# Tower layers over two tiles at a time, and one more sum on ScalarE, in an interaction network with a ranking tower

## The chip, the cores and the metric

The kernel runs on one core of a Trainium2 chip. The metric is the device time of one execution in microseconds, the median of several.

## The reference

For 1024 samples, 32 embedding rows of 16 numbers are gathered, three cross layers are applied, and a small tower follows. Everything is fp32.

```python
# x0, e: (1024, 32, 16); W0: (32, 32, 64); W1, W2: (32, 64, 64)
for W in (W0, W1, W2):
    xk = relu(einsum('bmd,bhd,mhk->bkd', x0, xk, W))
    outs.append(sum(xk, axis=2))            # over d
h = concatenate(outs + [dense_ctx], axis=1)  # 3 * 64 + 16 columns
h = maximum(h @ W_top1 + b_top1, 0)          # 208 x 512
h = maximum(h @ W_top2 + b_top2, 0)          # 512 x 256
y = h @ W_top3                               # 256 x 1
```

## The kernel before

The batch is cut into 16 streams of 64 samples (COLS = 64 x 16 = 1024 columns of sample and d). Two streams, an even one a (slot a) and an odd one b (slot b), make a tile of 128 samples (TB). A layer of a stream is a sum over 16 chunks (4 in layer 0): VectorE or GpSimd multiplies a rolled copy of x0 (`rolled`) by xk into `zd` or `zg`, and TensorE multiplies the product by the chunk's weights into `acc`, the two halves of 512 columns into two halves of the partitions of one bank. VectorE makes two chunks with one instruction into one of three buffers (ZD_BUFS), GpSimd one chunk into one of four. Layer 0 has one more term, from the squares of x0 that ScalarE makes (`squares`). Layer 0 of every stream uses the bank `stage`, layers 1 and 2 a bank for each slot.

ORDER is the order of the phases, written by hand: for m = 0 to 6, with a = 2m + 2 and b = a + 1, it is (b - 2, 2, 0), (a, 0, 0), (b - 2, 2, 1), (a, 1, 0), (b, 0, 0), (a, 1, 1), (b, 1, 0), (a, 2, 0), each (stream, layer, part). TensorE, VectorE and GpSimd all go through it. A pass of the loop over m is these eight phases, and the last phase (15, 2, 0) stands alone.

After a layer ScalarE copies relu(acc) to `xk_ps` for VectorE and `xk_sb` for GpSimd (`evacuate`, L486). It then sums relu over d for each sample with 32 activations of 16 columns that accumulate (`sum_d`, L465). Where `by_act` says no, it writes relu to `relu_ab` (L498) and VectorE reduces it (`reduce_d`, L391). In the passes of m this is layer 0 of slot a alone. Before a stream starts, ScalarE copies `base` (x0 repeated) for VectorE (`base_to_ps`, L439). Each phase of TensorE waits until the sums over its bank are done.

The tower of a tile runs as three blocks in TensorE's queue, in a bank of its own (`mlp`): `mlp2(m - 1)` in the phase (a, 1, 0), `mlp3(m - 1)` in (a, 1, 1), `mlp1(m)` in (b, 1, 0) after its fourth item. ScalarE takes each result out (`h2_to_sb`, `y_to_sb`, `h1_to_sb`). The sums come to it by six copies (`zsum_to_sb`). Tile 7 has code of its own at the end.

SP's queue issues, for each stream, a store of the gathered rows to a scratch (L269), a load of `base` (L287), and 16 loads of rolled tiles (L296). Each of these waits until the user before it (the same slot's layer 2) has used the tile (L294). GpSimd issues the gathers between its products.

## Time and profile before

| | |
|---|---|
| median of 3 runs | 613.49 us (612.25 to 613.73) |
| the profiled execution | 612.87 us |
| its span | 611.1 us, mean granted clock 0.992 |
| TensorE busy | 559.8 us |
| VectorE busy | 549.2 us |
| GpSimd busy | 451.9 us |
| ScalarE busy | 406.4 us |

The span is the time from the first to the last instruction, so 1.8 us of the profiled execution lie around it. The rows further down name engines as PE (TensorE), PEld (its weight loads), DVE (VectorE), ACT (ScalarE), POOL (GpSimd) and SPq (SP's queue). Each fp32 matmul is recorded twice, as two records.

### The profile page before, as it was taken

To read this page: it belongs to the slowest core of one execution; us is meant where nothing else is said; L and a number is where in the kernel's file an instruction comes from. 1 tells how busy PE (TensorE), PEld (TensorE's weight loads), DVE (VectorE), ACT (ScalarE), POOL (GpSimd) and SP (SyncE) were. 2 spreads that over 40 slices of the span, in tenths; PEclk is the share of its full clock that TensorE was granted. 3 is DMA by queue.
4 is the path that set the end of the run, shared out by engine and by line. 5 is a ranking of instruction groups with operands and counts; after the bars stand their busy time and mean duration, and the time that the engine had idled before them with its cause. 6 is when DMAs were issued, how large, how long until landed. Compare 5 with 4: busy or idle time off the path is not lost.

```text
span 611.1 us, 9367 instructions
## 1 busy us (share of the span) xinstructions
PE 559.8 (92%) x2668; PEld 201.3 (33%) x2668; DVE 549.2 (90%) x267; ACT 406.4 (67%) x2717; POOL 451.9 (74%) x347
## 2 busy tenths in 40 slices
PE   0058889999999999999999999999999999999997
PEld 0012322323333343344333343343334333333344
DVE  0077799999999999999999999999999999999990
ACT  0031506677877688768867688778867688678851
POOL 6748788878888878888888888888887874214630
PEclk9998899999999999999999999999999999999999
DMA  6297969693598819895597819894598819891000
GB/s 173 81 386 260 392 238 393 230 398 123 168 399 295 326 38 365 286 388 185 168 400 286 335 43 390 289 401 138 193 380 284 330 50 388 294 413 46 2 1 1
DMA packets 54263, 152.11 MB, mean 249 GB/s; under 512 B 9697, under 2 KB 18913, under 8 KB 54210
## 3 DMA queue, kind: packets, MB, share of 16 engines
q1 hardware_dynamic: 46018, 149.39, 65.3%
q0 software_dynamic: 8192, 2.11, 2.8%
q8 instruction: 21, 0.34, 0.2%
q14 instruction: 32, 0.26, 0.1%
HBM read 147.26 MB, written 4.20 MB: 248 GB/s over the span
## 4 chain that ended last, share of the span: by engine, by line
PE 82%; DVE 6%; POOL 5%; issue 3%; DMA 2%; ACT 1%; SPq 1%; DVEq 0%; POOLq 0%
PE acc L606 74%; DVE zd L415 6%; POOL emb L332 4%; PE mlp L643 2%; PE acc L615 2%; DMA rolled<-x_scratch 2%; PE mlp L634 1%; PE mlp L635 1%; POOL zg L344 1%; SPq L296 1%; PE mlp L650 1%; ACT xk_sb L486 0%; DMA emb<-tables_in,index 0%; ACT xk_ps L486 0%; DMA x_scratch<-emb 0%
## 5 line engine op out<-in xcount | busy, mean ns | idle before, releaser
L415 DVE TENSOR_TENSOR zd<-rolled,xk_ps 128x2048 f32<-128x2048 f32 (+1 forms) x246 | 535.4, 2248 | 14.1 <-PE acc L606 11.6
L606 PE MATMUL acc<-zd,w_sb 128*64 128x512 f32 x1700 | 388.8, 597 | 8.5 <-DVE zd L415 8.5
L332 POOL DMA_INDIRECT emb<-tables_in,index x256 | 244.5, 955 | 77.2 <-issue 64.7
L344 POOL TENSOR_TENSOR zg<-rolled,xk_sb 128x1024 f32<-128x1024 f32 x87 | 207.2, 2384 | 57.1 <-ACT xk_sb L486 41.6
L606 PEld LDWEIGHTS acc<-zd,w_sb 128*64 128x64 f32 x1700 | 120.5, 138 | 254.9 <-issue 219.5
L465 ACT ACTIVATE relu_ab<-acc 128x16 f32<-128x16 f32 x1152 | 190.9, 302 | 3.8 <-PE acc L606 3.5
L465 ACT ACTIVATION_READ_ACCUMULATOR relu_ab<-acc 128x1 f32 x1152 | 191.6, 329 | 0.1
L486 ACT ACTIVATE xk_sb<-acc 64x512 f32<-64x512 f32 x128 | 76.4, 597 | 57.5 <-PE acc L606 55.0
L606 PE MATMUL acc<-zd,w 128*64 128x512 f32 x256 | 62.8, 610 | 36.5 <-DVE zd L415 36.5
L606 PE MATMUL acc<-zg,w_sb 128*64 128x512 f32 x348 | 90.9, 600 | 2.9 <-POOL zg L344 2.8
L486 ACT ACTIVATE xk_ps<-acc 64x512 f32<-64x512 f32 x126 | 71.8, 570 | 28.0 <-PE acc L606 25.1
L443 ACT ACTIVATE xk_sb<-base 128x1024 f32<-128x1024 f32 x16 | 16.9, 1057 | 57.0 <-PE acc L606 28.7
L606 PEld LDWEIGHTS acc<-zd,w 128*64 128x64 f32 x256 | 18.6, 140 | 71.4 <-issue 69.3
L606 PEld LDWEIGHTS acc<-zg,w_sb 128*64 128x64 f32 x348 | 24.5, 137 | 50.5 <-issue 44.3
L439 ACT COPY xk_ps<-base 128x512 f32<-128x512 f32 x30 | 16.6, 587 | 23.7 <-DMA base<-x_scratch 18.7
L415 DVE TENSOR_TENSOR zd<-rolled,base 128x1024 f32<-128x1024 f32 x4 | 4.9, 1230 | 27.7 <-DMA rolled<-x_scratch 27.7
L615 PE MATMUL acc<-xk_sb,w 128*64 128x512 f32 x64 | 18.3, 648 | 0.0
L643 PEld LDWEIGHTS mlp<-h,wt 128*128 128x128 f32 x112 | 13.0, 191 | 5.7 <-issue 5.7
L391 DVE TENSOR_REDUCE zpart<-relu_ab 128x32 f32<-128x512 f32 x12 | 8.1, 678 | 7.0 <-ACT relu_ab L498 7.0
L643 PE MATMUL mlp<-h,wt 128*128 128x128 f32 x112 | 14.4, 281 | 0.0
L498 ACT ACTIVATE relu_ab<-acc 128x512 f32<-128x512 f32 x12 | 7.2, 598 | 7.3 <-PE acc L606 7.0
L515 ACT ACTIVATE h<-mlp,bt 128x128 f32<-128x128 f32 x28 | 8.0, 368 | 5.7 <-PE mlp L635 5.7
(45 smaller groups left out, 88.0 us busy)
## 6 DMA issues: line engine op xcount, KB each, us to landing
rolled<-x_scratch SPq DMA_DIRECT2D x256, 512.0 KB, 10.5
base<-x_scratch SPq DMA_DIRECT2D x16, 512.0 KB, 3.7
emb<-tables_in,index POOLq DMA_INDIRECT x256
x_scratch<-emb SPq DMA_DIRECT2D x32, 128.0 KB, 5.9
w_sb<-w_in SPq DMA_DIRECT2D x2, 512.0 KB, 4.6
wt<-wtop_in SPq DMA_DIRECT2D x1, 512.0 KB, 6.6
wt1a<-wtop_in SPq DMA_DIRECT2D x1, 256.0 KB, 5.2
w<-w0a_in SPq DMA_DIRECT2D x1, 160.0 KB, 2.3
```

The source lines that it names most:

```text
L332: pool.indirect_dma_start(emb[:, i % 2, c * DIM:(c + 1) * DIM], None, tables, bass.IndirectOffsetOnAxis(index[:, g:g + 1].bitcast(U32), 0) ...
L344: nc.gpsimd.tensor_tensor(zg[:, n % ZG_BUFS, :], rolled[:, s, j, :], xk_sb[:, s, :], ALU.mult).then_inc(zg_ready, 1)
L391: nc.vector.tensor_reduce(zpart[:, t % 2, layer, s, :], relu_ab[:, s, :].rearrange("p (b d) -> p b d", d=DIM), AX_X, ALU.add).then_inc(red ...
L415: nc.vector.tensor_tensor(zd[:, n % ZD_BUFS, 0:w, :], rolled[:, s, j:j + w, :], repeated(layer_in, w), ALU.mult).then_inc(zd_ready, 1)
L439: nc.scalar.copy(xk_ps[:, s, h * HALF:(h + 1) * HALF], base[:, h * HALF:(h + 1) * HALF]).then_inc(base_ps, 1)
L443: nc.scalar.activation(xk_sb[:, i % 2, :], base[:, :], ACT.Square).then_inc(squares_ready, 1)
L465: end = nc.scalar.activation(relu_ab[:, s, cols], acc[:, bank, cols], ACT.Relu, accum_out=zpart[:, t % 2, layer, s, b:b + 1])
L486: nc.scalar.activation(dst[copy * MAPS:(copy + 1) * MAPS, s, h * HALF:(h + 1) * HALF], acc[h * MAPS:(h + 1) * MAPS, bank, :], ACT.Relu).th ...
L515: nc.scalar.activation(h1[:, c, :], mlp[:, c * TB:(c + 1) * TB], ACT.Relu, bias=bt1[:, c:c + 1]).then_inc(h1_sb, 1)
L606: end = nc.tensor.matmul(acc[h * MAPS:(h + 1) * MAPS, bank, :], weights, z[:, h * HALF:(h + 1) * HALF], start=(j + c == 0), stop=(i == len ...
L615: nc.tensor.matmul(acc[h * MAPS:(h + 1) * MAPS, bank, :], w0[:, L0CH, :], xk_sb[:, s, h * HALF:(h + 1) * HALF], start=False, stop=False)
L643: end = nc.tensor.matmul(mlp[:, c * TB:(c + 1) * TB], wt2[:, k, c * P:(c + 1) * P], h1[:, k, :], start=(k == 0), stop=(k == H1 // P - 1))
```

## The change

The tower takes two tiles (256 columns, TW) at a time for tiles 0 to 5, and tile 6 alone as before. The first layer has 4 x 256 columns of output, twice the bank, so it is done in two halves: part 0 in the phase (b, 1, 0) and part 1 in (a, 2, 0), both in odd m, with ScalarE emptying the bank between them. The second and third layer of the pair are done in the next pass, which has an even m > 0. ScalarE sums layer 0 of slot a as well, from stream 2 on, so VectorE's reductions in the passes of m are gone. To make room, `index` is computed in place in `ids_sb`, `h2` lies in one half of `relu_ab`, and all sums of streams after 0 write their unread output to the other half.

```diff
+TW = 2 * TB
+PAIRS = (TILES - 2) // 2
 def by_act(stream, layer):
     if stream < 2:
         return layer == 2
-    return (layer > 0 or stream % 2 == 1) and (stream, layer) != (STREAMS - 1, 2)
+    return (stream, layer) != (STREAMS - 1, 2)
...
-        index = sb("index", [P, STREAMS * GATHERS], I32)
+        index = ids_sb[:, 1:]
...
-        z01 = sb("z01", [P, TB])
+        z01 = sb("z01", [P, TW])
-        h1 = sb("h1", [P, H1 // P, TB])
-        h2 = sb("h2", [P, H2 // P, TB])
+        h1 = sb("h1", [P, H1 // P, TW])
+        h2 = relu_ab[:, 0, :].rearrange("p (c b) -> p c b", b=TW)
...
             def reduce_d(q):
                 stream, layer, _ = ORDER[q]
                 s, t = stream % 2, stream // 2
-                if layer == 0 and s == 0 and t > 1:
-                    dve.wait_ge(zsum_sb, ZSUM_COPIES * (t - 1))
...
             def sum_d(stream, layer):
-                before = phase_before(stream, layer)
-                if by_act(*before):
-                    act.wait_ge(summed, act_sums_to(*before))
+                unread = relu_ab[:, min(stream, 1), :]
+                if stream == 0:
+                    act.wait_ge(reduced, sums_to(0, 1))
                 else:
-                    act.wait_ge(reduced, sums_to(*before))
+                    act.wait_ge(reduced, sums_to(1, 1))
+                    act.wait_ge(summed, act_sums_to(stream, layer) - 1)
...
+            def h1_to_sb(p, part):
+                act.wait_ge(h1_done, 2 * p + part + 1)
+                for x in range(2):
+                    c = 2 * part + x
+                    nc.scalar.activation(h1[:, c, :], mlp[:, x * TW:(x + 1) * TW], ACT.Relu,
+                                         bias=bt1[:, c:c + 1]).then_inc(h1_sb, 1)
...
             for t in range(1, TILES):
                 a, b, m = 2 * t, 2 * t + 1, t - 1
+                first_of_two, second_of_two = m % 2 == 0 and m > 0, m % 2 == 1
                 base_to_ps(a)
                 wait_end(a - 2, 2)
                 squares(a)
                 sum_d(a - 2, 2)
                 evacuate(a, 0)
                 base_to_ps(b)
+                sum_d(a, 0)
                 wait_end(b - 2, 2)
                 squares(b)
                 sum_d(b - 2, 2)
-                if m > 0:
-                    h2_to_sb(m - 1)
+                if first_of_two:
+                    h2_to_sb(m // 2 - 1)
                 evacuate(b, 0)
                 zsum_to_sb(m)
-                if m > 0:
-                    y_to_sb(m - 1)
+                if first_of_two:
+                    y_to_sb(m // 2 - 1)
                 sum_d(b, 0)
                 evacuate(a, 1)
-                h1_to_sb(m)
+                if second_of_two:
+                    h1_to_sb(m // 2, 0)
+                elif m == TILES - 2:
+                    one_h1_to_sb()
                 sum_d(a, 1)
                 evacuate(b, 1)
                 sum_d(b, 1)
+                if second_of_two:
+                    h1_to_sb(m // 2, 1)
...
+            def mlp1(p, part):
+                if part == 0:
+                    pe.wait_ge(zsum_sb, ZSUM_COPIES * (2 * p + 2))
+                    if p > 0:
+                        pe.wait_ge(y_ready, p)
+                else:
+                    pe.wait_ge(h1_sb, 4 * p + 2)
+                for x in range(2):
+                    c, dst = 2 * part + x, mlp[:, x * TW:(x + 1) * TW]
+                    nc.tensor.matmul(dst, wt1a[:, c * P:(c + 1) * P], z01[:, :], start=True, stop=False)
+                    end = nc.tensor.matmul(dst, wt1b[:, c * P:(c + 1) * P], z2d[:, p * TW:(p + 1) * TW],
+                                           start=False, stop=True)
+                end.then_inc(h1_done, 1)
...
             for m in range(TILES - 1):
-                q = 6 + 8 * m
+                q, p = 6 + 8 * m, m // 2
+                first_of_two, second_of_two = m % 2 == 0 and m > 0, m % 2 == 1
                 for x in range(3):
                     phase(q + x)
-                phase(q + 3, {1: lambda: mlp2(m - 1)} if m > 0 else {})
+                phase(q + 3, {1: lambda: mlp2(p - 1)} if first_of_two else {})
                 phase(q + 4)
-                phase(q + 5, {4: lambda: mlp3(m - 1)} if m > 0 else {})
-                phase(q + 6, {3: lambda: mlp1(m)})
-                phase(q + 7)
-            m = TILES - 2
-            phase(len(ORDER) - 1, {1: lambda: mlp2(m), 4: lambda: mlp3(m), 6: last_sums})
+                phase(q + 5, {4: lambda: mlp3(p - 1)} if first_of_two else {})
+                if m == TILES - 2:
+                    phase(q + 6, {3: one_mlp1})
+                else:
+                    phase(q + 6, {3: lambda: mlp1(p, 0)} if second_of_two else {})
+                phase(q + 7, {3: lambda: mlp1(p, 1)} if second_of_two else {})
+            phase(len(ORDER) - 1, {1: one_mlp2, 4: one_mlp3, 6: last_sums})
```

`mlp2`, `mlp3`, `h2_to_sb` and `y_to_sb` are as before with TW in place of TB. `one_mlp1`, `one_mlp2`, `one_mlp3` and their copies are the old code for tile 6. `zsum_to_sb(m)` writes its columns of the wide `z01`.

## Rows read from the trace of the kernel before

**Rows 1.** The page: busy time of each engine.

```profile
PE 559.8 (92%) x2668; PEld 201.3 (33%) x2668; DVE 549.2 (90%) x267; ACT 406.4 (67%) x2717; POOL 451.9 (74%) x347
```

**Rows 2.** By stretch (m = 0, 3): length; busy PE, PEld, DVE, ACT, POOL; clock; DMA.

```profile
84.69:153.17 68.48, 65.43 (x298) 20.85 (x298) 68.48 (x34) 41.38 (x238) 56.98 (x47) 1.00 0.77 281
...
290.14:358.63 68.49, 68.49 (x335) 24.88 (x336) 67.52 (x33) 53.38 (x372) 59.21 (x47) 1.00 0.75 273
```

**Rows 3.** TensorE's waits in m = 0 (84.69 to 153.17): total, times, longest.

```profile
PE acc L606 <- DVE zd L415: 3.9, 12, 0.9
```

**Rows 4.** VectorE's waits for TensorE in m = 3 (290.14 to 358.63).

```profile
DVE zd L415 <- PE acc L606: 0.6, 1, 0.6
```

**Rows 5.** Timeline of TensorE, m = 3: start, us, instruction, count.

```profile
332.64 0.60 PE L606 MATMUL acc<-zd,w_sb 128*64 128x512 f32 x2
333.17 2.05 PE L643 MATMUL mlp<-h,wt 128*128 128x128 f32 x16
335.15 0.65 PE L606 MATMUL acc<-zd,w 128*64 128x512 f32 x2
...
339.50 3.60 PE L606 MATMUL acc<-zd,w_sb 128*64 128x512 f32 x16
342.93 1.03 PE L606 MATMUL acc<-zg,w_sb 128*64 128x512 f32 x4
...
346.79 0.60 PE L606 MATMUL acc<-zd,w_sb 128*64 128x512 f32 x2
347.32 0.60 PE L650 MATMUL mlp<-h,wt 128*1 128x128 f32 x4
347.85 0.65 PE L606 MATMUL acc<-zg,w_sb 128*64 128x512 f32 x2
```

**Rows 6.** Timeline of VectorE, m = 3, around its reduction.

```profile
326.18 0.68 DVE L391 TENSOR_REDUCE zpart<-relu_ab 128x32 f32<-128x512 f32 x1
326.78 2.27 DVE L415 TENSOR_TENSOR zd<-rolled,xk_ps 128x2048 f32<-128x2048 f32 x1
```

**Rows 7.** Table by stretch for the sums (L465) alone, m = 3.

```profile
290.14:358.63 68.49, 27.07 (x320) 1.00 0.75 273
```

**Rows 8.** Timeline of ScalarE, m = 3; in brackets idle time before, and releaser.

```profile
326.78 1.11 ACT L439 COPY xk_ps<-base 128x512 f32<-128x512 f32 x2 [0.96 <-DMA base<-x_scratch]
...
339.71 2.44 ACT L486 ACTIVATE xk_sb<-acc 64x512 f32<-64x512 f32 x4 [3.03 <-PE acc L606]
...
347.96 0.25 ACT L526 COPY z2d_y<-mlp 1x128 f32<-1x128 f32 x1 [1.82 <-PE mlp L650]
```

**Rows 9.** Timelines of VectorE, then TensorE, m = 4, around (11, 1, 0).

```profile
417.25 4.47 DVE L415 TENSOR_TENSOR zd<-rolled,xk_ps 128x2048 f32<-128x2048 f32 x2
...
417.25 5.75 PE L606 MATMUL acc<-zd,w_sb 128*64 128x512 f32 x26
```

**Rows 10.** Timelines of VectorE's waits in m = 1 and 4, and TensorE ahead of the second.

```profile
155.08 2.29 DVE L415 TENSOR_TENSOR zd<-rolled,xk_ps 128x2048 f32<-128x2048 f32 x1 [0.15 <-PE acc L606]
...
429.04 2.29 DVE L415 TENSOR_TENSOR zd<-rolled,xk_ps 128x2048 f32<-128x2048 f32 x1 [0.73 <-PE acc L606]
...
427.06 0.65 PE L606 MATMUL acc<-zd,w_sb 128*64 128x512 f32 x2
```

**Rows 11.** Timeline of VectorE, its waits for a rolled tile, m = 3 and 5.

```profile
333.84 2.29 DVE L415 TENSOR_TENSOR zd<-rolled,xk_ps 128x2048 f32<-128x2048 f32 x1 [0.39 <-DMA rolled<-x_scratch]
...
470.69 2.29 DVE L415 TENSOR_TENSOR zd<-rolled,xk_ps 128x2048 f32<-128x2048 f32 x1 [0.26 <-DMA rolled<-x_scratch]
```

**Rows 12.** Timeline of SP's queue, m = 3: start and time of issuing.

```profile
296.57 12.51 SPq L296 DMA_DIRECT2D rolled<-x_scratch  x16
309.12 1.07 SPq L269 DMA_DIRECT2D x_scratch<-emb  x2
322.84 0.52 SPq L287 DMA_DIRECT2D base<-x_scratch  x1
```

**Rows 13.** Table by stretch between store and base load, m = 3; columns of rows 2.

```profile
309.00:322.80 13.80, 13.80 (x68) 4.65 (x66) 13.80 (x7) 9.10 (x71) 12.21 (x10) 1.00 0.92 351
```

More of the change, by code:

```diff
@@ L464, in sum_d @@
                     cols = slice(b * DIM, (b + 1) * DIM)
-                    end = nc.scalar.activation(relu_ab[:, s, cols], acc[:, bank, cols], ACT.Relu,
+                    end = nc.scalar.activation(unread[:, cols], acc[:, bank, cols], ACT.Relu,
                                                accum_out=zpart[:, t % 2, layer, s, b:b + 1])
@@ L492, in evacuate @@
                 if before and by_act(*before):
-                    act.wait_ge(summed, act_sums_to(*before))
+                    act.wait_ge(summed, act_sums_to(stream, layer))
                 elif before:
@@ L503, in zsum_to_sb @@
                 act.wait_ge(summed, act_sums_to(2 * m + 1, 2))
-                if m > 0:
-                    act.wait_ge(h1_done, m)
-                for layer, dst in enumerate([z01[0:MAPS, :], z01[MAPS:P, :], z2d[0:MAPS, m * TB:(m + 1) * TB]]):
+                if m > 1:
+                    act.wait_ge(h1_done, 2 * (m // 2))
+                col = m % 2 * TB
+                for layer, dst in enumerate([z01[0:MAPS, col:col + TB], z01[MAPS:P, col:col + TB],
+                                             z2d[0:MAPS, m * TB:(m + 1) * TB]]):
                     for h in range(2):
@@ new lines, in mlp2, with mlp3 @@
+            def mlp2(p):
+                pe.wait_ge(h1_sb, 4 * (p + 1))
+                for c in range(H2 // P):
+                    for k in range(H1 // P):
+                        end = nc.tensor.matmul(mlp[:, c * TW:(c + 1) * TW], wt2[:, k, c * P:(c + 1) * P],
+                                               h1[:, k, :], start=(k == 0), stop=(k == H1 // P - 1))
+                end.then_inc(h2_done, 1)
+            def mlp3(p):
+                pe.wait_ge(h2_sb, 2 * (p + 1))
+                for k in range(H2 // P):
+                    end = nc.tensor.matmul(mlp[0:1, 0:TW], wt3[:, k:k + 1], h2[:, k, :],
+                                           start=(k == 0), stop=(k == H2 // P - 1))
+                end.then_inc(y_done, 1)
@@ L632, in mlp1, with one_mlp1 @@
+            def one_mlp1():
+                pe.wait_ge(zsum_sb, ZSUM_COPIES * (TILES - 1))
+                pe.wait_ge(y_ready, PAIRS)
                 for c in range(H1 // P):
                     dst = mlp[:, c * TB:(c + 1) * TB]
-                    nc.tensor.matmul(dst, wt1a[:, c * P:(c + 1) * P], z01[:, :], start=True, stop=False)
-                    end = nc.tensor.matmul(dst, wt1b[:, c * P:(c + 1) * P], z2d[:, m * TB:(m + 1) * TB],
-                                           start=False, stop=True)
+                    nc.tensor.matmul(dst, wt1a[:, c * P:(c + 1) * P], z01[:, 0:TB], start=True, stop=False)
+                    end = nc.tensor.matmul(dst, wt1b[:, c * P:(c + 1) * P],
+                                           z2d[:, (TILES - 2) * TB:(TILES - 1) * TB], start=False, stop=True)
@@ L637, in mlp1, with one_mlp2 @@
                 end.then_inc(h1_done, 1)
-            def mlp2(m):
-                pe.wait_ge(h1_sb, 4 * (m + 1))
+            def one_mlp2():
+                pe.wait_ge(h1_sb, 4 * (PAIRS + 1))
                 for c in range(H2 // P):
@@ L643, in mlp2, with one_mlp3 @@
                         end = nc.tensor.matmul(mlp[:, c * TB:(c + 1) * TB], wt2[:, k, c * P:(c + 1) * P],
-                                               h1[:, k, :], start=(k == 0), stop=(k == H1 // P - 1))
+                                               h1[:, k, 0:TB], start=(k == 0), stop=(k == H1 // P - 1))
                 end.then_inc(h2_done, 1)
-            def mlp3(m):
-                pe.wait_ge(h2_sb, 2 * (m + 1))
+            def one_mlp3():
+                pe.wait_ge(h2_sb, 2 * (PAIRS + 1))
                 for k in range(H2 // P):
-                    end = nc.tensor.matmul(y_bank, wt3[:, k:k + 1], h2[:, k, :],
+                    end = nc.tensor.matmul(mlp[0:1, 0:TB], wt3[:, k:k + 1], h2[:, k, 0:TB],
                                            start=(k == 0), stop=(k == H2 // P - 1))
@@ L680, in _ @@
             for c in range(H1 // P):
-                nc.tensor.matmul(last_h1_bank[c], wt1a[:, c * P:(c + 1) * P], z01[:, :], start=True, stop=False)
-            pe.wait_ge(y_ready, m)
+                nc.tensor.matmul(last_h1_bank[c], wt1a[:, c * P:(c + 1) * P], z01[:, 0:TB], start=True, stop=False)
+            pe.wait_ge(y_ready, PAIRS + 1)
             pe.wait_ge(reduced, sums_to(STREAMS - 1, 2))
@@ L691, in _ @@
                 for c in range(H2 // P):
-                    end = nc.tensor.matmul(last_h2_bank[c], wt2[:, k, c * P:(c + 1) * P], h1[:, k, :],
+                    end = nc.tensor.matmul(last_h2_bank[c], wt2[:, k, c * P:(c + 1) * P], h1[:, k, 0:TB],
                                            start=(k == 0), stop=(k == H1 // P - 1))
@@ L697, in _ @@
                 pe.wait_ge(last_h2_sb, k + 1)
-                end = nc.tensor.matmul(last_y_bank, wt3[:, k:k + 1], h2[:, k, :],
+                end = nc.tensor.matmul(last_y_bank, wt3[:, k:k + 1], h2[:, k, 0:TB],
                                        start=(k == 0), stop=(k == H2 // P - 1))
```

46 lines of the change are left out of this document (24 added, 22 removed).

## The prediction

> **What bounds the kernel now.** I read the page's busy shares first: TensorE is busy 92% and VectorE 90% of the span [rows 1]. The table by stretch splits this [rows 2]. In the pass m = 3 TensorE is busy for all 68.49 us and VectorE for 67.52, and the other passes from m = 1 to 5 are like it. In the first pass (m = 0) it is the other way round: VectorE is busy for all 68.48 us and TensorE for 65.43. So two engines are within 1.5% of each other, and the question is not only how much work TensorE loses but when it has it. The waits say the same: in the pass m = 0, which has no second and third tower layer in it, TensorE waits 12 times for VectorE's products [rows 3]; in the pass m = 3 VectorE waits instead, 0.6 us for TensorE [rows 4] and 0.39 for a transfer [rows 11]. The clock is granted in full in both [rows 2], so all TensorE times below are at 2.4 GHz.
>
> **Sizes of the blocks.** TensorE's work in one pass is 74 chunks, as ORDER and CHUNKS have them, and three tower blocks. A chunk (two halves, two records each) takes 0.858 us: 16 records in 3.43 us (339.50 to 342.93) [rows 5], which is 0.429 per 512 columns, and the two halves of a pair run together. In the second tower layer 16 records lie between 333.17 and 335.15 [rows 5]. The records stand 0.1115 us apart (1.98 less the 0.2 up to the next chunk, over 16). Counted from the last chunk's second record (332.64, and 0.43 for its streaming) the block costs TensorE 2.08 us, and 2.13 with the slower start of the chunk behind it. The first layer is the same size, 2.13. The third layer (347.32 to 347.85, last record before it 346.79) costs 0.68 [rows 5]. Of each block some 0.25 to 0.35 us is not streaming.
>
> **What the change takes and gives on TensorE.** With twice the columns I price a record at 0.2158 us: 128 columns take 0.1115 and 512 take 0.429, and a straight line between them gives 0.217. Then half a first layer for two tiles is 8 x 0.2158 + 0.35 = 2.08, the second layer 16 x 0.2158 + 0.35 = 3.80, the third 4 x 0.2158 + 0.25 = 1.11. A pair costs 2.08 x 2 + 3.80 + 1.11 = 9.07 where two tiles cost 2 x (2.13 + 2.13 + 0.68) = 9.88. That is 0.81 less per pair, 2.4 us over three pairs. The block's fixed part is bounded by zero and 0.35, which moves a pair by 0.3 at most in its path below. The Trainium skill's page "TensorE: Matmul & The Clock Gate" (Back-to-back issue gap) gives a sustained spacing of about 81 ns at 128 columns and 131 ns at 512; the rows have 111.5 and 429, so here four times the columns cost 3.8 times and not 1.6 times. By the page's ratio, a record of 256 columns would cost an estimated 0.135 us.
>
> **VectorE and ScalarE.** VectorE loses one reduction per pass: 326.18 to 326.78, 0.60 us [rows 6]. ScalarE gets a sixth sum per pass: 27.07 us for five is 5.41 each [rows 7], less the 0.6 copy that it replaces. ScalarE is busy 53.4 of 68.5 us [rows 2] and would be at about 58, which fits. I followed it in the pass m = 3: it copies base for the odd stream from 326.78 for 1.1 us [rows 8], sums until 333.3, and then squares. TensorE begins that stream's first layer at 335.15, behind the tower's second layer [rows 5]. With that layer gone it could begin at 333.1, so 0.2 us late, at a place where it is about to wait for VectorE anyway. The odd stream's relu copies start at 339.7 after a wait of 3.03 us [rows 8], and are then on time. The copy of y is waited for 1.8 us [rows 8], in passes with a third layer only. I price ScalarE at nothing. Its cover is these waits, and without them it would cost up to 2 us in a pass. GpSimd gets nothing new. VectorE's queue also loses its wait for the z copies, which held nothing.
>
> **When TensorE has the work.** Now a second and third layer for two tiles stand in the passes m = 2, 4, 6 ("first"), both halves of a first layer in m = 1, 3, 5 ("second"). A second pass therefore loses 2.13 + 0.68 = 2.81 us of TensorE work ahead of the middle of the odd stream's layer 1, where TensorE has almost nothing in hand. In the pass m = 4 it starts the third item of (11, 1, 0) at 422.40 (12 steps of 0.429 after 417.25), and VectorE ended that product at 421.72, so the lead is 0.68 [rows 9]. The smallest lead that the trace needs is about 0.06. VectorE has 0.6 us less to do and 2.81 is taken, so TensorE waits 2.81 - 0.62 - 0.6, about 1.6 us, there. In a first pass the long second layer holds VectorE instead, for all three product buffers are then full: the same product starts at 419.44, TensorE had freed its buffer at 418.97, and the tightest that occurs is 0.21 (a start at 429.04 after a release at 428.83, which is 427.06 and four steps, a wait of 0.73) [rows 9, 10]. That leaves 0.26.
>
> So the longest path alternates. From the third product of (b, 1, 0) in a second pass it runs on TensorE, past the two half blocks, into the first pass, past the long second and third layers. There it passes to VectorE's third product of (b, 1, 0), and VectorE works without a wait until the same place of the next second pass. Against before, for one pair:
> - TensorE: +4.16 - 2.13 (two halves for one block), +1.67 (3.80 - 2.13), +0.43 (1.11 - 0.68) = +4.13
> - room at the handover to VectorE -0.26, and at the one back -0.62
> - VectorE: reduction -0.60, its wait of 0.73 gone.
>
> That is +1.92 us per pair. Ahead of it stands the opening. VectorE sets m = 0 and m = 1, and at the handover in m = 1 it is earlier by two reductions, the 0.15 that it waited at 155.08 [rows 10] and the room of 0.62, 1.97 in all; the two halves for one block then give back 2.03. That is +0.06 by the end of m = 1. Then come two pairs of passes (m = 2, 3 and 4, 5), and m = 6, which keeps its own first layer and pays +1.67 + 0.43 = +2.10; TensorE leads from there to the end. Sum: 0.06 + 2 x 1.92 + 2.10 = +6.0 us.
>
> **The transfer.** In a second pass a DMA chain runs beside VectorE: the even stream's 16 rolled tiles are issued from 296.57, as VectorE frees them, the store of the odd stream's scratch queues behind them (309.12), its base load follows at 322.84, and VectorE's second product of (9, 0, 0) waits until 333.84 for its tile [rows 11, 12]. DMA is 92% busy between the store and the base load [rows 13], so I hold the 37.3 us from issue to landing fixed. VectorE then can't use its 0.6 there, nor the 0.39 that it waits already: +1.0 us in m = 3. In m = 5 the wait is 0.26 [rows 11], so +0.86. In m = 1 there is no such wait, but VectorE comes 0.75 earlier, and I add 0.2. Together +2.0. It is between 0 (the chain follows) and 2.0, and I take the whole, for its start is set by VectorE's own releases. The forecast is +8.0 on the profiled execution's 612.87 us, so 620.9; the median of before is 0.6 above that execution, so 621.5.
>
> **Rivals.**
> - The transfers follow VectorE: +6.0, 619.5 us. For it: m = 1, 4 and 6 show no such wait. Against it: the 92%.
> - ScalarE is late as well. Its new sum stands ahead of the squares and of the odd stream's sum, and with a base load that lands at 326.7 it has no idle time until 339. At 1 us in each second pass and 0.5 in the first ones, 624 us. It decides once its relu copies start later than TensorE's end plus the 3.0 us shown.
> - It gets faster: TensorE's lead isn't used up, and its own work sets the time. That is 2.4 us off plus 0.6 for the reduction in m = 0: 610.5 us. It needs VectorE to make its products faster than one per 2.2 us when not held. The pass m = 0 speaks against it, for TensorE waited there and VectorE was still busy without a break [rows 2, 3].
> - Wide records are cheap and the long blocks stay short. With a record of 256 columns no dearer than one of 128, the path per pair is 1.24 x 2 - 2.13 - 2.21 = -1.86, the opening -1.62: 608 us. By the Trainium skill's ratio above it would be an estimated 611. The 3.8 times speaks against both.
>
> **Numbers.** The forecast has 0.5, the following transfers 0.22, late ScalarE 0.13, the two faster rivals 0.07 and 0.03; 0.05 is left for a gain and a loss that meet. The range from 616.5 to 624.5 holds the first three, with fixed parts of the blocks near zero at its low end. 0.3% is 1.8 us, about what this kernel's runs can tell. Faster 0.09, same 0.05, slower 0.86.
>
> **What would show it.** In the changed profile: TensorE waits for VectorE's products in m = 1, 3, 5, 2.7 us for a pair and 1.0 more where the transfer binds (the 1.92 and the 0.81 that it has less to do), and hardly in m = 2, 4, 6; VectorE waits for TensorE by some 4 us in m = 2, 4; passes of unequal length, and no reduction in either; tower blocks of 2.1, 2.1, 3.8 and 1.1 us. TensorE's waits in second passes under 0.5 us would make it wrong, or relu copies of ScalarE as the releaser of TensorE or VectorE.

## The result, and the profile after

The changed kernel takes 620.0 us (618.63 to 621.92, 4 runs) where the one before takes 612.87 (612.08 to 613.73, 4 runs). The ratio is 1.0122, interval [1.0106, 1.0137]: 7.1 us slower. The profiled execution took 621.92 us with a span of 620.1, against 612.87 and 611.1 before, so it is 9.0 us longer, and 1.9 above its own median. The forecast was 621.5, or 620.9 against the profiled 612.87.

The page's busy shares, to set beside [rows 1]:

```profile
PE 561.5 (91%) x2560; PEld 193.4 (31%) x2560; DVE 546.7 (88%) x260; ACT 434.3 (70%) x3137; POOL 451.7 (73%) x347
```

No engine of the two at the top got more work of note. TensorE's 561.5 is 1.7 more, but a record's time contains short waits, so its work is better counted from block sizes, below. VectorE has 2.5 less. Both shares fell because the span grew. ScalarE has 27.9 more. From these shares alone no one could say why it is slower.

The table by stretch of the changed kernel can. Each row is one pass, m = 1 to 6, counted from TensorE's first item of (b - 2, 2, 0); columns as in [rows 2].

```profile
172.38:243.71 71.33, 69.23 (x315) 23.56 (x313) 68.57 (x32) 57.29 (x432) 61.45 (x49) 1.00 0.77 277
243.71:312.48 68.77, 68.64 (x319) 24.18 (x317) 66.45 (x31) 57.36 (x431) 55.59 (x44) 1.00 0.71 256
312.48:382.99 70.51, 69.30 (x315) 23.41 (x313) 68.48 (x32) 57.30 (x432) 61.24 (x47) 1.00 0.78 282
382.99:451.76 68.77, 68.64 (x319) 24.18 (x317) 66.44 (x31) 57.37 (x431) 58.15 (x47) 1.00 0.71 254
451.76:523.99 72.23, 69.31 (x315) 23.37 (x313) 68.57 (x32) 57.29 (x432) 52.82 (x35) 1.00 0.75 277
523.99:594.54 70.55, 70.55 (x334) 26.06 (x332) 67.25 (x31) 57.29 (x433) 27.43 (x12) 1.00 0.43 165
```

Two passes of the kernel before, cut at the same place:

```profile
174.60:243.09 68.49, 68.49 (x334) 24.89 (x332) 67.76 (x33) 53.39 (x372) 57.77 (x44) 1.00 0.74 271
243.09:311.58 68.49, 68.49 (x334) 24.89 (x332) 67.85 (x33) 53.38 (x372) 59.28 (x46) 1.00 0.75 273
```

Before, each of these passes takes 68.49. After, the passes with the first-layer halves (m = 1, 3, 5) take 71.33, 70.51 and 72.23, and TensorE's busy time in them is less than the pass. The passes with the second and third layer (m = 2, 4) take 68.77, with VectorE at only 66.45. So neither kind of pass uses both engines. Adding up against before: TensorE comes to the start of m = 2 at 243.71, which is 0.62 later. Then m = 2 and 3 give +2.30, m = 4 and 5 +4.02, m = 6 +2.06. The last phase, from 594.54, is as long as before (25.5). The sum is 9.0, all of the difference.

The table of waits shows who waits for whom. For TensorE in m = 1 to 5, then for VectorE from 84 to 594 us (total, times, longest):

```profile
PE acc L636 <- DVE zd L415: 5.9, 14, 1.9
```

```profile
DVE zd L415 <- PE acc L636: 12.6, 22, 1.3
DVE zd L415 <- DMA rolled<-x_scratch: 3.5, 5, 1.6
```

The clearest places are in VectorE's timeline. First one wait in a second pass and one in the first pass after it (m = 3, m = 4), then the waits for a rolled tile in m = 5:

```profile
378.12 2.29 DVE L415 TENSOR_TENSOR zd<-rolled,xk_ps 128x2048 f32<-128x2048 f32 x1 [1.27 <-PE acc L636]
...
410.18 2.29 DVE L415 TENSOR_TENSOR zd<-rolled,xk_ps 128x2048 f32<-128x2048 f32 x1 [1.24 <-PE acc L636]
...
473.14 2.29 DVE L415 TENSOR_TENSOR zd<-rolled,xk_ps 128x2048 f32<-128x2048 f32 x1 [1.61 <-DMA rolled<-x_scratch]
475.82 4.48 DVE L415 TENSOR_TENSOR zd<-rolled,xk_ps 128x2048 f32<-128x2048 f32 x2 [0.39 <-DMA rolled<-x_scratch]
```

The wait at 378.12 stands behind the second half block (which TensorE runs from 373.28 to 375.21), the one at 410.18 behind the long second layer: all three product buffers are full while TensorE is in the tower. The last of VectorE's waits for TensorE in m = 4 is this one:

```profile
424.16 4.49 DVE L415 TENSOR_TENSOR zd<-rolled,xk_ps 128x2048 f32<-128x2048 f32 x2 [0.33 <-PE acc L636]
```

It is the third product of (11, 1, 0). From there up to the second half block of m = 5 VectorE waits only for rolled tiles (and 0.1 us once), and TensorE waits for VectorE up to the third item of (13, 1, 0), which starts at 495.74. And the blocks themselves, TensorE's timeline around a half first layer (m = 1, L669 and L670), the second layer (L678) and the third (L685) in m = 2:

```profile
232.19 1.89 PE L636 MATMUL acc<-zd,w_sb 128*64 128x512 f32 x8
234.00 0.70 PE L669 MATMUL mlp<-z,wt1a 128*128 128x256 f32 x2
234.54 0.60 PE L670 MATMUL mlp<-z2d_y,wt1b 80*128 80x256 f32 x2
234.97 0.60 PE L669 MATMUL mlp<-z,wt1a 128*128 128x256 f32 x2
235.41 0.59 PE L670 MATMUL mlp<-z2d_y,wt1b 80*128 80x256 f32 x2
235.93 0.65 PE L636 MATMUL acc<-zg,w_sb 128*64 128x512 f32 x2
...
263.45 1.89 PE L636 MATMUL acc<-zd,w_sb 128*64 128x512 f32 x8
265.26 3.72 PE L678 MATMUL mlp<-h,wt 128*128 128x256 f32 x16
268.92 1.94 PE L636 MATMUL acc<-zd,w 128*64 128x512 f32 x8
...
277.55 3.60 PE L636 MATMUL acc<-zd,w_sb 128*64 128x512 f32 x16
281.08 1.02 PE L685 MATMUL mlp<-relu_ab,wt 128*1 128x256 f32 x4
282.04 1.08 PE L636 MATMUL acc<-zg,w_sb 128*64 128x512 f32 x4
```

The two chunks that start at 232.19 are done 4 x 0.429 = 1.72 later, at 233.91, and the next chunk starts at 235.93: the half block costs 2.02 us. In the same way the second layer costs 268.92 - (263.45 + 1.72) = 3.75 and the third 282.04 - (277.55 + 3.43) = 1.06. A record of 256 columns is (3.66 - 0.2) / 16 = 0.216 us. The Trainium skill's page "TensorE: Matmul & The Clock Gate" (Back-to-back issue gap) has about 81 ns at 128 columns and 131 ns at 512, by whose ratio a record of 256 columns would take an estimated 0.135 us here. The trace, with 0.216, does not agree with it for these fp32 records.

So TensorE's work in a second pass is 74 x 0.858 + 2 x 2.02 = 67.5 us, and in a first pass 63.5 + 3.75 + 1.06 = 68.3. Of m = 3's 70.51 us TensorE had nothing to do for 3.0, though the waits of m = 3 come to only 0.9 for products and 0.2 more in the trace. The rest must lie inside the records' own durations: those add up to 69.3, which is 1.8 above the work.

### The profile page after: what moved, and what is told of

Same layout as the page of the kernel before. It is cut to its first block, busy times and chain, and to the rows that moved or that the text cites. A ratio compares the mean times of both kernels' runs of the same rounds, so it can differ in the third digit from the quotient of the medians.

```text
span 620.1 us, 9569 instructions
## 1 busy us (share of the span) xinstructions
PE 561.5 (91%) x2560; PEld 193.4 (31%) x2560; DVE 546.7 (88%) x260; ACT 434.3 (70%) x3137; POOL 451.7 (73%) x347
## 4 chain that ended last, share of the span: by engine, by line
PE 56%; DVE 17%; DMA 9%; POOL 7%; issue 6%; ACT 2%; SPq 2%; DVEq 0%; POOLq 0%
PE acc L636 50%; DVE zd L415 17%; DMA rolled<-x_scratch 6%; POOL emb L335 5%; DMA x_scratch<-emb 2%; POOL zg L347 2%; SPq L299 2%; PE mlp L678 2%; PE mlp L669 1%; ACT relu_ab L467 1%; PE mlp L670 1%; PE acc L645 1%; ACT xk_sb L488 1%; PE mlp L685 0%; DMA emb<-tables_in,ids_sb 0%
## 5 line engine op out<-in xcount | busy, mean ns | idle before, releaser
L636 PE MATMUL acc<-zd,w_sb 128*64 128x512 f32 x1700 | 392.9, 598 | 12.8 <-DVE zd L415 12.5
L335 POOL DMA_INDIRECT emb<-tables_in,ids_sb x256 | 244.4, 955 | 78.3 <-issue 64.4
L467 ACT ACTIVATE relu_ab<-acc 128x16 f32<-128x16 f32 x1376 | 229.8, 339 | 4.1 <-PE acc L636 3.5
L467 ACT ACTIVATION_READ_ACCUMULATOR relu_ab<-acc 128x1 f32 x1376 | 230.5, 366 | 0.1
L443 ACT ACTIVATE xk_sb<-base 128x1024 f32<-128x1024 f32 x16 | 18.7, 1166 | 47.0 <-DMA base<-x_scratch 27.8
L636 PEld LDWEIGHTS acc<-zd,w 128*64 128x64 f32 x256 | 18.4, 138 | 76.8 <-issue 70.4
L521 ACT ACTIVATE h<-mlp,bt 128x256 f32<-128x256 f32 x12 | 5.8, 600 | 9.9 <-PE mlp L670 9.9
L678 PE MATMUL mlp<-h,wt 128*128 128x256 f32 x48 | 11.2, 386 | 0.0
L678 PEld LDWEIGHTS mlp<-h,wt 128*128 128x128 f32 x48 | 8.9, 190 | 3.5 <-issue 2.4
L391 DVE TENSOR_REDUCE zpart<-relu_ab 128x32 f32<-128x512 f32 x5 | 3.4, 679 | 7.0 <-ACT relu_ab L500 7.0
L645 PEld LDWEIGHTS acc<-xk_sb,w 128*64 128x64 f32 x64 | 5.2, 143 | 9.4 <-issue 9.4
## 6 DMA issues: line engine op xcount, KB each, us to landing
x_scratch<-emb SPq DMA_DIRECT2D x32, 128.0 KB, 11.4
```

Source lines behind the costliest of these rows:

```text
L335: pool.indirect_dma_start(emb[:, i % 2, c * DIM:(c + 1) * DIM], None, tables, bass.IndirectOffsetOnAxis(index[:, g:g + 1].bitcast(U32), 0) ...
L443: nc.scalar.activation(xk_sb[:, i % 2, :], base[:, :], ACT.Square).then_inc(squares_ready, 1)
L467: end = nc.scalar.activation(unread[:, cols], acc[:, bank, cols], ACT.Relu, accum_out=zpart[:, t % 2, layer, s, b:b + 1])
L636: end = nc.tensor.matmul(acc[h * MAPS:(h + 1) * MAPS, bank, :], weights, z[:, h * HALF:(h + 1) * HALF], start=(j + c == 0), stop=(i == len ...
L645: nc.tensor.matmul(acc[h * MAPS:(h + 1) * MAPS, bank, :], w0[:, L0CH, :], xk_sb[:, s, h * HALF:(h + 1) * HALF], start=False, stop=False)
L678: end = nc.tensor.matmul(mlp[:, c * TW:(c + 1) * TW], wt2[:, k, c * P:(c + 1) * P], h1[:, k, :], start=(k == 0), stop=(k == H1 // P - 1))
```

## The experiments

Three chips were used. e1 to e4 ran on one, e5 to e7 and later e11 and e12 on a second, e8 to e10 on a third; the result's own chip isn't noted. Ratios are against the kernel before on the same chip; its medians there were 612.63, 613.74 (613.39 beside e11 and e12) and 613.96 us.

**e1: the new sums on the tower of before.** ScalarE sums layer 0 of slot a, VectorE's reduction is gone, the tower is as before.

```diff
 def by_act(stream, layer):
-    return (layer > 0 or stream % 2 == 1) and (stream, layer) != (STREAMS - 1, 2)
+    return (stream, layer) != (STREAMS - 1, 2)
...
                 base_to_ps(b)
+                sum_d(a, 0)
                 wait_end(b - 2, 2)
```

> The tower stays one tile at a time; ScalarE alone takes over the sums of layer 0 of slot a. Theory (TensorE sets the passes from m = 1 on, VectorE only m = 0): the reduction removed in m = 0 gives 0.6 us, those removed later go into VectorE's waits (about 1.3 us a pass in place of 0.7), so 612.9 - 0.6 = 612.3 us. Rival (ScalarE's sixth sum holds the others): ScalarE late by 1 us in each pass, about 618 us, which would make the sum and not the wide tower the cause.

Measured: 611.75 us, 0.9982 [0.9973, 0.9991]. TensorE sets most passes then (m = 4: 68.46 us of work and of pass), so VectorE's 0.6 less is worth next to nothing there, and ScalarE's sum costs nothing. The loss is not in the sums, on this chip. Counted like the passes above, e1 comes to m = 1 2.0 us earlier than before, but its m = 2 and 3 take 69.33 and 68.72, with 1.5 and 0.9 us of VectorE's waits for rolled tiles in them. So the transfers bind here too, once VectorE has less to do, and take back half of what the opening gave.

**e2: a thin tower.** On the kernel before, tiles 0 to 6 compute one chunk of each layer instead of all.

```diff
-                for c in range(H1 // P):
+                for c in range(1):
...
-                for c in range(H2 // P):
-                    for k in range(H1 // P):
+                for c in range(1):
+                    for k in range(1):
...
-                for k in range(H2 // P):
+                for k in range(1):
```

> The kernel before with only one matmul pair (first layer) and one matmul (second, third layer) in each tower block of tiles 0 to 6; ScalarE's copies stay, so y of these tiles is left wrong. TensorE loses about 3.2 us of its 4.9 us of tower work in each of seven passes. Theory (VectorE has only 0.73 us of waits in a pass to give): TensorE waits in every pass and the time falls by about 0.7 us a pass, to 608 us. Rival (TensorE's work alone sets the time): 22 us less, 591 us.

Measured: 607.15 us, 0.9904 [0.989, 0.9918]. The table by stretch of e2, m = 1:

```profile
173.26:240.92 67.66, 66.69 (x307) 21.27 (x304) 67.66 (x33) 53.39 (x372) 58.24 (x45) 1.00 0.75 278
```

Here VectorE is busy for the whole pass, and the pass is 67.66. With most of the tower gone the kernel gains 0.8 us in such a pass and no more. VectorE is a floor just under TensorE, as [rows 2] had it. (Two of e2's later passes take 68.6 and 69.1; TensorE waits for GpSimd's products in them, 2.8 us in four waits.)

**e3: a filler in the second passes.** The changed kernel, with 8 more records of 256 columns in TensorE's queue in m = 1, 3 and 5, where before the second layer stood. Nothing reads their result.

```diff
+            def filler(p):
+                if p > 0:
+                    pe.wait_ge(y_ready, p)
+                for x in range(2):
+                    for k in range(2):
+                        nc.tensor.matmul(mlp[:, x * TW:(x + 1) * TW], wt2[:, k, 0:P], wt2[:, k, :],
+                                         start=(k == 0), stop=(k == 1))
...
-                phase(q + 3, {1: lambda: mlp2(p - 1)} if first_of_two else {})
+                phase(q + 3, {1: lambda: mlp2(p - 1)} if first_of_two else {1: lambda: filler(p)} if second_of_two else {})
```

> The changed kernel with four more matmuls of 256 columns (2.1 us of TensorE work that nothing reads) behind the second item of phase (a, 1, 0) in the passes m = 1, 3, 5. Theory: TensorE waits more than 2 us for VectorE in just this stretch, so the work is hidden, 620 us give or take 1. Rival (TensorE's own work sets these passes): 3 x 2.1 more, 626 us.

Measured: 619.91 us, 1.011 [1.0095, 1.0125], no longer than the changed kernel at 1.0122. TensorE's timeline in m = 3 of e3 has the filler; TensorE's waits in m = 1 to 5 and VectorE's from 84 to 594 us follow:

```profile
332.45 1.89 PE L636 MATMUL acc<-zd,w_sb 128*64 128x512 f32 x8
334.27 1.99 PE L695 MATMUL mlp<-wt 128*128 128x256 f32 x8
336.19 1.94 PE L636 MATMUL acc<-zd,w 128*64 128x512 f32 x8
```

```profile
PE acc L636 <- DVE zd L415: 0.7, 3, 0.3
```

```profile
DVE zd L415 <- PE acc L636: 12.6, 22, 1.3
DVE zd L415 <- DMA rolled<-x_scratch: 1.7, 2, 1.1
```

The filler takes 336.19 - (332.45 + 1.72) = 2.02 us, three times 6.1 us in all. TensorE's waits for products fell from 5.9 to 0.7, and the time did not move. So TensorE idles about 2 us in each second pass, between the place of the filler and the middle of stream b's layer 1, which is the place that the prediction named. VectorE's waits for TensorE are the same to the digit (12.6, 22 times).

**e4: the same wide tower, spread evenly.** For the pairs p = 0 and 1 the second half of the first layer moves from (a, 2, 0) of the second pass to (a, 1, 0) of the first pass, the two output chunks of the second layer to (b, 1, 0) of that pass and (a, 1, 0) of the next, and the third layer behind them. The pair of tiles 4 and 5 stays as in the change, for tile 6 comes right after it.

```diff
-                phase(q + 3, {1: lambda: mlp2(p - 1)} if first_of_two else {})
-                phase(q + 4)
-                phase(q + 5, {4: lambda: mlp3(p - 1)} if first_of_two else {})
...
+                elif first_of_two:
+                    at3, at6 = {1: lambda: mlp1(p - 1, 1)}, {3: lambda: mlp2(p - 1, (0,))}
+                elif second_of_two:
+                    if p > 0:
+                        at3, at5 = {1: lambda: mlp2(p - 1, (1,))}, {4: lambda: mlp3(p - 1)}
+                    at6 = {3: lambda: mlp1(p, 0)}
+                    if p == 2:
+                        at7 = {3: lambda: mlp1(p, 1)}
+                phase(q + 3, at3)
+                phase(q + 4)
+                phase(q + 5, at5)
+                phase(q + 6, at6)
+                phase(q + 7, at7)
```

> Two tiles at a time with the blocks spread for the first two pairs: second half of the first layer in phase (a, 1, 0) of the even pass, the second layer in two halves (even pass (b, 1, 0), odd pass (a, 1, 0)), the third layer in (a, 1, 1) of the odd pass. TensorE's work in the tower is 0.35 us more than in the changed kernel per pair. Theory (the loss is from when TensorE has the work): by the same bookkeeping -2.0 at the end of m = 1, -0.8 in m = 2, +0.3 in m = 3, -0.8 in m = 4, +2.4 in m = 5, which keeps the old place of the half block, +2.1 in m = 6: about +1.2, 614 us. Rival (the wide matmuls or ScalarE's sums cost it wherever they stand): 620 us or more.

Measured: 614.86 us (613.56 to 616.63), 1.0037 [1.0023, 1.005]. The table by stretch of e4, m = 1 to 6:

```profile
172.52:240.91 68.39, 67.14 (x307) 22.16 (x305) 67.96 (x32) 56.43 (x430) 59.14 (x47) 1.00 0.76 280
240.91:308.98 68.07, 67.89 (x314) 23.85 (x312) 67.35 (x32) 57.10 (x431) 58.96 (x46) 1.00 0.76 273
308.98:377.76 68.78, 68.78 (x318) 23.97 (x316) 67.44 (x32) 57.57 (x432) 59.51 (x47) 1.00 0.74 274
377.76:445.56 67.80, 67.80 (x315) 23.86 (x313) 67.39 (x32) 57.10 (x431) 58.51 (x47) 1.00 0.76 275
445.56:516.92 71.36, 71.07 (x326) 25.37 (x324) 67.99 (x32) 58.30 (x434) 53.02 (x35) 1.00 0.75 273
516.92:587.48 70.56, 70.56 (x335) 26.06 (x332) 67.25 (x31) 57.12 (x433) 27.42 (x12) 1.00 0.43 166
```

The passes m = 1 to 4 now take 273.0 us together, against 279.4 in the change and 274.0 before. The same matmuls, placed evenly, save 5 us of e3's 619.91, which stands for the changed kernel on this chip, its filler being hidden. What is left over stands in m = 5 and 6, which were not spread and take 141.9 where before took 137.0.

**e5: the changed kernel again**, unedited, on the second chip, beside e6 and e7.

> The changed kernel once more, as the control of the two beside it on one chip. Both theories: 620 us (618.6 to 622).

Measured: 628.86 us (624.84 to 630.61), 1.0241 [1.0213, 1.0268]. This missed by 9 us: on this chip the change costs 15 us, twice as much, while the kernel before takes only 1.1 us more than on the first chip (613.74 against 612.63). The groups of ScalarE's sums show what differs (busy and mean ns, then idle time before them and its releaser). The changed kernel of the result first, then e5:

```profile
L467 ACT ACTIVATION_READ_ACCUMULATOR relu_ab<-acc 128x1 f32 x1376 | 230.5, 366 | 0.1
```

```profile
L467 ACT ACTIVATION_READ_ACCUMULATOR relu_ab<-acc 128x1 f32 x1376 | 231.4, 291 | 12.1 <-issue 12.1
L467 ACT ACTIVATE relu_ab<-acc 128x16 f32<-128x16 f32 x1376 | 229.3, 267 | 12.6 <-issue 8.2 <-PE acc L636 3.5
```

```profile
336.24 0.18 ACT L467 ACTIVATE relu_ab<-acc 128x16 f32<-128x16 f32 x1 [0.45 <-issue]
336.95 0.20 ACT L467 ACTIVATION_READ_ACCUMULATOR relu_ab<-acc 128x1 f32 x1 [0.52 <-issue]
```

The last fence is from e5's timeline of ScalarE, in the new sum of layer 0. There are gaps between its 64 small instructions in which it waits for nothing that the profile shows. Without gaps a sum of 32 takes 5.4 us from its first instruction to the end of its last (median of the 43 of the result's trace, longest 5.65); in e5 the median is 5.9 and the longest 8.6. In e5's waits from 84 to 540 us TensorE now waits for those sums too:

```profile
PE acc L636 <- issue: 6.6, 10, 2.3
PE acc L636 <- DVE zd L415: 4.5, 13, 0.9
PE acc L636 <- ACT relu_ab L467: 4.3, 5, 1.8
```

Most of what e5 loses does not stand in the second passes. Beside the profiled execution of the result it comes to m = 1 2.9 us later, and its first passes take 70.1 and 70.4 where those took 68.8; its second passes take 71.6, 71.3 and 70.5 where those took 71.3, 70.5 and 72.2.

**e6 and e7: half the rolled tiles' bytes.** For the even streams from 2 on, only 512 of the 1024 columns of a rolled tile are loaded (the rest keeps old data), in the changed kernel (e6) and in the kernel before (e7).

```diff
-                        sp.dma_start(rolled[:, s, j, :], rows_from(BASES[j], i, 1)).then_inc(rolled_in[s][j], 16)
+                        cols = HALF if s == 0 and i > 1 else COLS
+                        sp.dma_start(rolled[:, s, j, 0:cols], bass.AP(
+                            scratch.tensor, scratch.offset + (i * ROWS + BASES[j]) * COLS,
+                            [[COLS, FIELDS], [COLS, GROUPS], [1, cols]])).then_inc(rolled_in[s][j], 16)
```

> The changed kernel, but the 16 rolled loads of every even stream from 2 on bring only the first 512 of 1024 columns (the other half of the tile is stale, so the output of these streams is left wrong). Theory (in the odd passes VectorE waits for the odd stream's base and rolled tiles, which queue behind these loads, 2.0 us over the three passes): about 2 us less than the control, 618 us, and no wait of VectorE for base or rolled tiles from m = 1 to 5. Rival (the transfers would follow VectorE, or its waits are absorbed by waits for TensorE): 620 us as the control.

> The kernel before with the same halved loads. Theory (TensorE sets its passes from m = 1 on, and VectorE's waits for tiles only replace waits for TensorE): 612.6 us, no change. Rival (its own transfers bound it as well): 1 us less or more.

Measured: e6 626.08 us, 1.0194 [1.0178, 1.021], 2.8 us under e5 and with no wait of VectorE for a rolled tile; e7 613.89, 0.9999 [0.9985, 1.0013]. So fewer bytes helped the changed kernel and not the one before. But e5's trace has only 0.4 us of such waits, the intervals of e5 and e6 all but touch, and the gaps fill the same slack. That is support for the transfer term, not proof of its size.

**e8, e9, e10: the two halves of the change apart, on a chip with gaps.** e8 is the wide tower with the sums of before (the unread output goes to the bank itself, for want of room). e9 is the changed kernel again, e10 is e1 again.

```diff
 def by_act(stream, layer):
-    return (stream, layer) != (STREAMS - 1, 2)
+    return (layer > 0 or stream % 2 == 1) and (stream, layer) != (STREAMS - 1, 2)
...
-                unread = relu_ab[:, min(stream, 1), :]
+                unread = acc[:, bank, :]
...
-                sum_d(a, 0)
```

> The wide tower alone: layer 0 of slot a is reduced by VectorE again, as in the kernel before. (To make room, the sums of ScalarE write their unread output back into PSUM, with a wait for its own copies ahead of it.) Theory (the loss is the wide tower's blocks against VectorE's products; the reduction keeps VectorE 0.6 us longer in each pass): opening +1.3, each pair +2.5, m = 6 +2.1, transfers +0.7, 9 us over the kernel before, 622 us, on any chip. Rival (the new sum on ScalarE is what costs): 614 us.

> The changed kernel as the control on this chip. On a chip where ScalarE's sums take 5.3 us each: 620 us, 2 less than the wide tower alone. On one where ScalarE's instructions come with gaps inside the sums (5.8 to 8.6 us each, as in the two wide runs before this one): 626 to 629 us, so 4 to 7 more than the wide tower alone.

> The narrow tower with ScalarE's new sum, again. Where ScalarE's sums take 5.3 us: 611.8 us (0.18% under the kernel before). Where they come with gaps: ScalarE has 11 us of idle time in a pass here and the tower's second layer still covers the start of the odd stream, so the same 0 to 1 us under the kernel before; if ScalarE's lateness counted by itself, 3 us over it.

Measured: e8 622.48 us, 1.0154 [1.013, 1.0178]; e9 628.91, 1.0242 [1.0203, 1.0281]; e10 623.23, 1.0155 [1.013, 1.018]. The wide tower alone costs 8.5 us here, near what it would cost without gaps if the two halves add up (the change's 7.1 and the 0.9 that e1 gained make 8.0); no run has the wide tower alone on a chip without gaps. e8 has gaps too, and its TensorE waits 1.4 us for sums. The new sums alone cost 9.3 here, where on the first chip they gained 0.9: e10 missed its expectation widely. Both together cost 15.0, less than the sum of 17.8; presumably one wait covers part of the other. The waits of e10 from 84 to 540 us, for TensorE and then for ScalarE:

```profile
PE acc L604 <- DVE zd L412: 7.2, 16, 1.3
PE acc L604 <- issue: 2.8, 6, 1.3
PE acc L604 <- ACT relu_ab L462: 1.3, 1, 1.3
```

```profile
ACT relu_ab L462 <- issue: 17.9, 42, 1.4
```

e1's TensorE waited 3.0 us for products in the same stretch. In e10 VectorE waited 4.6 us for ScalarE's relu copies, in e1 never. So a late sum delays the relu copies behind it in ScalarE's queue, these VectorE's products, and those TensorE.

In e9 the clock takes a part as well. TensorE idles 2.84 us behind a sum that is late, and 1 us after it has gone on the granted clock is at the lower level, 1.2 GHz (0.50 in the table by stretch, columns as in [rows 2]):

```profile
339.78 2.83 PE L636 MATMUL acc<-zd,w 128*64 128x512 f32 x8 [2.84 <-ACT relu_ab L467]
```

```profile
341.00:344.00 3.00, 3.00 (x8) 0.73 (x6) 2.03 (x2) 2.86 (x37) 2.54 (x3) 0.50 1.02 388
```

The eight records took 2.83 us where the same eight take 1.94 in the result's trace. It happens again behind a wait of 2.21 us at 483.75, but not in e5 behind one of 2.28. e9's m = 3 takes 73.8 us and e5's 71.3. Of e9's six runs the two fastest have a mean granted clock of 0.997, the other four 0.989 to 0.992.

**e11 and e12: VectorE made shorter, in one kind of pass only.** On the second chip, in the changed kernel, two of VectorE's products of the phase (a, 1, 1) are made over half their columns (the rest of the buffer is old), in the second passes (e11) or in the first passes (e12).

```diff
-                    nc.vector.tensor_tensor(zd[:, n % ZD_BUFS, 0:w, :], rolled[:, s, j:j + w, :],
-                                            repeated(layer_in, w), ALU.mult).then_inc(zd_ready, 1)
+                    short = (layer, _part) == (1, 1) and x < 2 and stream % 4 == 0 and stream > 0
+                    cols = HALF if short else COLS
+                    nc.vector.tensor_tensor(zd[:, n % ZD_BUFS, 0:w, 0:cols], rolled[:, s, j:j + w, 0:cols],
+                                            repeated(layer_in[:, 0:cols], w), ALU.mult).then_inc(zd_ready, 1)
```

e12 has `stream % 4 == 2 and stream > 2`.

> The changed kernel, with the first two products of VectorE in phase (a, 1, 1) made over 512 of the 1024 columns, in the odd passes m = 1, 3, 5 only: 2.1 us less of VectorE's work in each (the other half of the product is stale, so the output of these streams is left wrong). Theory (in these passes VectorE's products set the time up to the third of (b, 1, 0)): 1.6 to 2.1 us less in each of the three, so 5 to 6 us less than the same cut in the even passes, which is the control: 615 us where the sums of ScalarE come without gaps, some 8 more where they have them. Rival (TensorE's work sets the odd passes): no difference to the control.

> The same cut of two products in the even passes m = 2, 4, 6 only. Theory (there VectorE waits for TensorE behind the long second layer, so what it saves goes into the wait): no change against the changed kernel, 620 us without gaps in ScalarE's sums, 628 with them. Rival (VectorE sets the even passes too, or all passes alike): as much less as with the cut in the odd passes.

Measured: e11 624.79 us, 1.0183 [1.0162, 1.0205]; e12 627.22, 1.0229 [1.0209, 1.0248]. The sign is as expected, and the size is not: 2.4 us apart where 5 to 6 were expected. In e11's m = 3 TensorE starts stream 9 after an idle time with no product to blame:

```profile
338.82 1.94 PE L638 MATMUL acc<-zd,w 128*64 128x512 f32 x8 [1.24 <-issue]
```

In ScalarE's timeline the last instruction of the new sum there starts at 338.42 and takes 0.35, so it ends as TensorE goes on. With gaps the late sum holds TensorE there too, which may be why a shorter VectorE helps only in part. The two traces don't show where the 2.4 us lie: e11's second passes take 71.0, 71.1 and 70.8, e12's 71.6, 70.8 and 71.1. e11's profiled execution is 1.1 above its median and has a wait of 2.0 for a rolled tile, and e12's is 2.2 below its own. So the pair supports the forecast by the sign of the medians alone. Over the kernel before, e12 costs 13.8 us and e11 11.4 where e5 cost 15.1 on the same chip, so 1.3 and 3.7 less (the intervals of e5 and e12 overlap); nothing and 5 to 6 were expected.

## Why the prediction was right, point by point

**Two engines take turns.** Right, and shown. The filler that costs nothing (e3) shows TensorE idle in second passes, the thin tower (e2) shows VectorE's floor, and spreading the same work (e4) gives most of the loss back. The handovers stand where the prediction put them, at the third product of (b, 1, 0) in both kinds of pass: VectorE's last wait for TensorE in m = 4 is there (424.16), and TensorE's last waits in m = 1, 3 and 5 are there too (215.46, 354.74, 495.74). "Its own work sets the time" (610.5 us) falls with this: TensorE's work per pair shrank and the time grew. What was saved was to be had here only when placed evenly: e4's m = 1, 2 and 4 take 68.39, 68.07 and 67.80, all below the 68.49 of before.

**Block sizes.** 2.02, 3.75 and 1.06 us where 2.08, 3.80 and 1.11 were priced: each 0.05 to 0.06 too dear, all in the fixed part. A pair is 8.85, so 1.03 less than two tiles by the old sizes. The rival of cheap wide records falls: 0.216 us was both priced and found. One bound in this step was wrong: fixed parts of zero would take 3 x 0.35 + 0.25 = 1.3 us off the path of a pair, not 0.3 at most. Measured, they took 0.22 off.

**The path per pair.** The prediction had +1.92. With the measured blocks its sum is 0.22 lower, +1.70: (4.04 - 2.13) + (3.75 - 2.13) + (1.06 - 0.68) = 3.91 where +4.13 stood. Measured are +2.30 and +4.02, with VectorE's waits for rolled tiles in m = 3 and 5 of 0.4 and 2.0. Less those waits they are 1.9 and 2.0, so the handovers, taken from two leads of 0.26 and 0.62, are good to 0.3 us. e3 gives the same 2.0 for both pairs. That the path comes out at the forecast's own +1.92 is luck in part: blocks 0.22 too dear and handovers 0.2 to 0.3 too roomy make up for each other. (One of those 0.3 is a reading: the wait of 0.73 that falls away is m = 4's, m = 2's is 0.58.) m = 6 was +2.10 and is +2.06.

**The opening.** +0.06 was forecast, and 0.2 for the transfer; measured is +0.62. The trace has 1.1 us of waits for rolled tiles in m = 1, where the one before has none. With the blocks as measured that would make -0.06 + 1.1 = 1.0, so some 0.4 of these waits did not reach TensorE's start of m = 2.

**The transfer.** Right in kind; this is the mis-sized term. +2.0 was the forecast, with 1.0 in m = 3, 0.86 in m = 5 and 0.2 in m = 1. The profiled execution has 0.4, 2.0 and 1.1, 3.5 in all. The path without transfers, with measured blocks, is -0.06 + 2 x 1.70 + 2.00 = 5.3 us, and with the 3.5 it is 8.8 of the 9.0 measured; two misses of 0.2 to 0.3 us in the pairs and the 0.4 of the opening nearly cancel in it. e3 gives the same account: 5.3 plus its 1.7 of transfer waits is 7.0, and its span is 618.3 - 611.1 = 7.2 longer. By this the waits for transfers differ by some 2 us between executions, which would also put the profiled one 1.9 above its median. That is read from traces and not shown by an experiment, for the direct test (e6) was blurred by the gaps. Against the rival "the transfers follow" it stays undecided how much follows: the medians are 7.1 apart, between its 6.0 and the forecast's 8.0.

**What was to be seen.** TensorE waits in m = 1, 3 and 5 and hardly in m = 2 and 4: so it is. "2.7 us for a pair and 1.0 more": for m = 2 and 3 TensorE's work is 67.5 + 68.3 = 135.8 and the passes take 139.3, so 3.5 us. VectorE's wait of some 4 us: 2.40 in m = 2, and 1.5 more already in the second pass, behind its second half block.

**ScalarE at nothing.** Right for the result and for e1, and wrong as a general statement. Even in the result's trace the sum had no room left. In m = 3 its last instruction, then TensorE's start of stream 9, which waits for that sum and for VectorE's first product (done at 334.45):

```profile
333.96 0.46 ACT L467 ACTIVATION_READ_ACCUMULATOR relu_ab<-acc 128x1 f32 x1
```

```profile
334.60 1.94 PE L636 MATMUL acc<-zd,w 128*64 128x512 f32 x8 [0.24 <-issue]
```

The sum ends at 334.42, 0.03 us ahead of the product; behind it TensorE had two more waits of 0.25 us for products to give. The rival "ScalarE is late as well" had 0.13 and 624 us, at 1 us in each second pass and 0.5 in each first one. On two of three chips it is true and larger than that: 628.9 in e5 and e9. The step "which fits" counted ScalarE's work (58 of 68.5 us) and took each sum at 5.41 us, which is what its trace had; it didn't ask what the cover is worth when a sum takes 6 to 9. The forecast is right where there are no gaps. That the result was measured there is luck: 628.9 lies outside the range.

**A better version.** None holds on all chips. e1 is 0.2% faster than the kernel before where there are no gaps and 1.55% slower where there are. e4 is 0.4% slower without gaps and has not been run with them. The kernel before is the one to keep.

## What to carry to other kernels

When two engines are within a few per cent of each other, ask of every moved block when its engine gets the work, not only how much: here some 3 us less matmul over three pairs made 7 us more. The traces show VectorE waiting with its three buffers full behind the long blocks, and TensorE waiting for products where the blocks are missing; whether a fourth buffer would carry enough over wasn't tested. If small blocks must be merged into bigger ones, spread the parts until no pass is heavier than the other engine's floor. And test work that is moved to an "idle" engine on more than one chip when it is made of many tiny instructions.

## What the runs showed of the hardware that was not expected

The gaps in ScalarE's stream of tiny instructions were there on two chips and not on a third. In the result's traces and on the first chip a pair of a 16-column activation and its accumulator read comes every 0.16 us without a break (0.1 us idle before 1376 reads). On the other two chips 20 to 23 us of such idle time stand in the changed kernel's stretch from 84 to 540 us (e5: 20.3 in 44 pieces of up to 1.2 us; e9: 23.4 in 47), in nothing but "issue". e7, which has the 36 sums of before, also shows gaps (9.1 us in 20 pieces). The kernel before takes 613.4 to 614.0 on those chips and 612.6 on the first, so its slack hides most of them; the sixth sum of each pass, at a place with little slack, does not hide.

What the engine lacks in these gaps the profile doesn't say. They are not scattered at random: 27 of e5's 44 stand in the same sum as a gap of e9, on another chip, and within 4 of its 64 instructions. Of the runs made side by side on one chip all had them or none did, whatever the kernel (e7 and e8, with the sums of before, had them too), and the second chip had them both times. So they go with the chip and not with the change, as far as four groups of runs on three chips can tell, and with a place in the stream of instructions. Whether the instructions themselves come late stays open.
